# One 128x512 product per head, with its own signal, in place of four 128x256 scalings in a cross-attention stage

## The chip, the cores and the metric

The kernel runs on one core of a Trainium2 chip. The metric is the device time of one execution in microseconds (us); the median of three runs before the change is 2084.72 us (2083.55 to 2086.55).

## The reference, cut to what matters

The program is a block of four layers, each a cross attention and a feed-forward network on x of shape (8, 256, 256), with a layer norm ahead of each and a gated residual behind it. The change touches only the second layer's cross attention: 16 heads of width 64, eight batches, 256 queries and 256 keys each.

```python
def _L1_xattn_ref(x, context, mask, Wq, Wk, Wv, Wo, bo):
    q = (x @ Wq).reshape(b, n, h, d)
    k = (context @ Wk).reshape(b, m, h, d)
    v = (context @ Wv).reshape(b, m, h, d)
    sim = jnp.einsum('bihd,bjhd->bhij', q, k) * scale
    sim = jnp.where(mask[:, None, None, :], sim, neg)
    attn = jax.nn.softmax(sim, axis=-1)
    out = jnp.einsum('bhij,bjhd->bihd', attn, v)
    return out.reshape(b, n, h * d) @ Wo + bo
```

## The kernel before

The stages follow one another with a barrier of all engines between them. Inside a stage each engine has its own program, written out in full (no loop remains in this stage), and the engines meet through semaphores. An engine does its instructions in the order in which they are written, and an instruction whose semaphore isn't there yet holds up all that stand behind it.

`stage_cross_attention` works on 64 pairs of heads, 8 pairs (`PAIRS`) in each of 8 batches. For a pair g, with its two heads e_ = 0 and 1 and two tiles of 128 queries each (it = 0 and 1), the steps are:

- `scores`: TensorE forms q·k for both heads into two of the four PSUM banks `main` (line 1209). VectorE adds the mask, writes `scored` and the row maxima (line 1328, four instructions). ScalarE takes the exponential into `e` and sums each row through the accumulator into `sums` (line 1269, four instructions). `e` has the shape [128, 3, 2, 2, 256]: three slots, head, query tile, key.
- `normalise`: VectorE takes the reciprocal of the four sums (line 1336) and scales the four 128x256 blocks of `e` by them, in place (line 1341).
- `turn`: TensorE transposes the scaled weights, four 128x128 blocks a head, into the banks `turned` (line 1221); a head has a bank of its own. VectorE copies the first head's bank to `eT` (line 1350), ScalarE the second's (line 1282).
- `weigh`: TensorE multiplies by v into `av` (line 1234), VectorE copies the result to `aoT` (line 1358).

The function `walk` gives the order, the same on every engine: scores(g+1), then a slot for filler work, turn(g-1), another slot, weigh(g-2). In VectorE's program turn(g-1) ends with normalise(g), so a pair is scaled one step ahead of its transposes. The filler work of `between` belongs to neighbouring batches and is put at fixed slots: the transposes of the next batch's x in pair 0 (line 1179), its four q projections in pairs 1, 2, 4 and 5 (line 1189), the two output projections of the batch before in pairs 3 and 4 (line 1197, with the residual on VectorE at line 223), and the layer norm's last step in pair 5 (line 217). The first batch has no output projection to do, the last has no q projection.

GpSimd adds the bias to x at the start of the stage (line 1371, 16 instructions of 128x256), and then does the small steps of the layer norm (lines 182 and 185).

Of the kernel before, what the change touches and what calls it, by code (L numbers as in the profile page):

```python
# [12 lines left out]
P = 128  # L13
# [8 lines left out]
ALU = mybir.AluOpType  # L22
# [3 lines left out]
B, S, D = 8, 256, 256  # L26
# [194 lines left out]
def residual(nc, dve, core, gate, update, t, x_done):  # L221

    nc.vector.scalar_tensor_tensor(core.x[:, t, :], update, gate, core.x[:, t, :], ALU.mult, ALU.add  # L223
                                   ).then_inc(x_done, 1)
# [859 lines left out]
def stage_cross_attention(nc, core, ins):  # L1084
# [10 lines left out]
    with ExitStack() as ctx:  # L1095
# [11 lines left out]
        neg_max, sums, rsums = (st.sb(n, [P, 2, 4]) for n in ("neg_max", "sums", "rsums"))  # L1107
        e = st.sb("e", [P, 3, 2, 2, S])
# [7 lines left out]
        exp_done, recip, norm_done = st.sem("exp_done"), st.sem("recip"), st.sem("norm_done")  # L1116
# [38 lines left out]
        @block.sync  # L1155
        def _(sp):
            sp.dma_start(wo[:, :, :], ins["L1_xattn_Wo"].rearrange("(k p) n -> p k n", p=P)).then_inc(wo_in, 16)
            for b in range(1, B):
                if b >= 2:
                    sp.wait_ge(av_done, PAIRS * (b - 1))  # L1160
                sp.dma_start(kT[b % 2][:, :, :].rearrange("p k s -> p (k s)"), kv.k_list[b, :, :]
                             ).then_inc(kv_in[b % 2], 16)
                sp.dma_start(v[b % 2][:, :, :].rearrange("p h n -> p (h n)"), kv.v_list[b, :, :]
                             ).then_inc(kv_in[b % 2], 16)

        @block.tensor
        def _(pe):
# [45 lines left out]
                            last.then_inc(filled, 1)  # L1213

            def turn(g):
                pe.wait_ge(norm_done, g + 1)
                for e_ in range(2):
                    ps, filled, eT_bank[g, e_] = wt.fill()
                    for jt in range(2):
                        for it in range(2):  # L1220
                            last = nc.tensor.transpose(ps[:, jt * S + it * P:jt * S + (it + 1) * P],  # L1221
                                                       e[:, g % 3, e_, it, jt * P:(jt + 1) * P], core.ident[:, :])
                    last.then_inc(filled, 1)

            def weigh(g):
# [11 lines left out]
                last.then_inc(av_done, 1)  # L1237

            walk(scores, fill, turn, weigh)

        @block.scalar
# [55 lines left out]
        @block.vector  # L1297
        def _(dve):
            wm, wt = Walk(main, dve), Walk(turned, dve)
            dve.wait_ge(small_in, 32)  # L1300
            nc.vector.tensor_scalar(mask_add[:, :, :].rearrange("p b s -> p (b s)"), mask8[:, :], -1.0, -NEG,
                                    ALU.add, ALU.mult).then_inc(mask_ready, 1)
            dve.wait_ge(mask_ready, 1)
            nc.vector.tensor_scalar(bias[:, :], bias[:, :], tg, None, ALU.mult).then_inc(bias_ready, 1)

            def fill(b, kind, n):
                if kind == "n":
                    for h in range(2):
                        norm.vector_apply(dve, 2 * b + h, h)
                elif kind == "o":  # L1310
                    ps, empty = wm.drain()
                    if b == 0 and n == 0:
                        dve.wait_ge(bias_added, TILES)
                    residual(nc, dve, core, tg, ps[:, 0:D], 2 * b + n, x_done)
                    norm.vector_stats(dve, 2 * b + n, n, x_done)
                    core.vector_inc(empty)
                else:
                    wm.skip(1)

            def scores(g):  # L1320
                b = g // PAIRS
                if g >= 2:
                    dve.wait_ge(exp_done, 4 * (g - 1))
                for e_ in range(2):
                    ps, empty = wm.drain()
                    for it in range(2):
                        n = 2 * e_ + it
                        last = nc.vector.tensor_tensor_reduce(  # L1328
                            scored[:, g % 2, e_, it, :], ps[:, it * S:(it + 1) * S], mask_add[:, b, :], -1.0, -NEG,
                            ALU.add, ALU.min, neg_max[:, g % 2, n:n + 1])  # L1330
                    last.then_inc(empty, 1)

            def normalise(g):
                par = g % 2
                dve.wait_ge(exp_done, 4 * (g + 1))
                nc.vector.reciprocal(rsums[:, par, :], sums[:, par, :]).then_inc(recip, 1)
                dve.wait_ge(recip, g + 1)
                for e_ in range(2):
                    for it in range(2):
                        n = 2 * e_ + it  # L1340
                        last = nc.vector.tensor_scalar(e[:, g % 3, e_, it, :], e[:, g % 3, e_, it, :],  # L1341
                                                       rsums[:, par, n:n + 1], None, ALU.mult)
                last.then_inc(norm_done, 1)

            def turn(g):
                ps, empty = wt.drain()
                wt.skip(1)
                if g >= 2:
                    dve.wait_ge(av_done, g - 1)
                nc.vector.tensor_copy(eT[:, g % 2, 0, :, :].rearrange("p j s -> p (j s)"), ps[:, :]  # L1350
                                      ).then_inc(empty, 1)
                if g + 1 < ALL_PAIRS:
                    normalise(g + 1)

            def weigh(g):
                b, p = divmod(g, PAIRS)
                dve.wait_ge(av_done, g + 1)
                nc.vector.tensor_copy(aoT[:, b % 2, p, :], ps_av[g % 2][:, 0:S]).then_inc(ao_ready, 1)

            def first_scores(g):  # L1360
                scores(g)
                if g == 1:
                    normalise(0)

            walk(first_scores, fill, turn, weigh)
# [2152 lines left out]
```

## Time and profile before

| what | before |
|---|---|
| median of three runs (lowest, highest) | 2084.72 us (2083.55, 2086.55) |
| the profiled execution's own time | 2084.0 us |
| its span in the trace | 2082.3 us |
| TensorE's mean granted clock | 0.952 of full speed |
| TensorE matmul, busy | 1875.5 us, 90% |
| VectorE, busy | 1270.4 us, 61% |
| ScalarE, busy | 834.9 us, 40% |
| GpSimd, busy | 274.3 us, 13% |
| the cross-attention stage | from 317 us to 659 us of the span |

Times in the trace are counted from the start of the span. An instruction's duration runs from its start to its end, and two VectorE instructions can overlap by some hundredths of a microsecond, so the step from one start to the next is what a queue pays. In a timeline, instructions of one kind that follow each other are merged: "x4" with 1.14 us is the time from the first one's start to the last one's end. Idle time stands in brackets, with the work whose end finished it. In the names a prefix tells the stage: `ca_` is the cross attention, `f_` the feed-forward stage before it, `bt_` the last stage of the program.

### The profile page before, as it was taken

What the parts mean: (1) busy time and instruction counts of PE and PEld (TensorE: products, weight loads), DVE (VectorE), ACT (ScalarE), POOL (GpSimd) and SP (SyncE); (2) the same over time, 40 slices, a digit from 0 to 9 for tenths busy, and PEclk for the clock granted to TensorE, in tenths of its full rate; (3) what the DMA queues carried; (4) which work ended last, traced back from release to release, by engine and by line L of the source; (5) the groups of instructions that cost most, each with busy time, mean ns of one, the idle gap of its engine ahead of it and who ended that gap; (6) DMA issues with size and microseconds to landing.
All of it is one profiled execution on the core that took longest, in us unless ns stands there. A gap on an engine that the chain in (4) does not pass through costs nothing. (4 is left out here: it accounts for less than half of the span.)

```text
span 2082.3 us, 39092 instructions
## 1 busy us (share of the span) xinstructions
PE 1875.5 (90%) x13707; PEld 1518.8 (73%) x13708; DVE 1270.4 (61%) x4668; ACT 834.9 (40%) x2278; POOL 274.3 (13%) x498
## 2 busy tenths in 40 slices
PE   8899997999998989999999988997952989999978
PEld 6566665677666979999999987875531877777745
DVE  7878865877874451111111145676769529999988
ACT  3433335655552111111111101774477524444468
POOL 2001112000001070000000063331000230000022
PEclk9999999999998999999999998999975999999989
DMA  6211112111113522222222021111000031111100
GB/s 224 87 51 51 41 51 74 44 79 41 41 42 102 201 80 81 86 86 83 83 86 86 23 65 45 44 45 62 0 0 0 1 93 40 39 37 39 23 11 31
DMA packets 106722, 124.95 MB, mean 60 GB/s; under 512 B 36160, under 2 KB 85832, under 8 KB 104776
## 3 DMA queue, kind: packets, MB, share of 16 engines
q1 hardware_dynamic: 95416, 107.25, 15.6%
q0 software_dynamic: 3072, 8.39, 1.3%
q10 hardware_dynamic: 8080, 7.35, 1.1%
q8 instruction: 85, 1.39, 0.3%
q14 instruction: 69, 0.57, 0.1%
HBM read 86.39 MB, written 36.63 MB: 59 GB/s over the span
## 5 line engine op out<-in xcount | busy, mean ns | idle before, releaser
L1781 DVE TENSOR_TENSOR me_h<-me_sg,me_ps_u 128x512 f32<-128x512 f32 x106 | 72.5, 687 | 287.1 <-PE me_ps_u L1604 274.0
L1737 ACT ACTIVATE me_sg<-me_ps_g 128x512 f32<-128x512 f32 x106 | 63.3, 597 | 370.1 <-PE me_ps_g L1604 340.2
L1269 ACT ACTIVATE ca_e<-ca_scored,ca_neg_max 128x256 f32<-128x256 f32 x256 | 127.2, 499 | 108.3 <-DVE ca_neg_max L1328 108.3
L1604 PE MATMUL me_ps_g<-me_x_turned,me_w 128*128 128x128 f32 x1184 | 144.6, 275 | 1.9 <-issue 1.9
L1604 PE MATMUL me_ps_u<-me_x_turned,me_w 128*128 128x128 f32 x1184 | 144.3, 275 | 0.0
L1604 PEld LDWEIGHTS me_ps_g<-me_x_turned,me_w 128*128 128x128 f32 x1184 | 140.7, 192 | 4.5 <-issue 2.8
L1611 PE MATMUL me_ps_y<-me_w,me_h 128*128 128x256 f32 x592 | 140.0, 379 | 0.0
L1604 PEld LDWEIGHTS me_ps_u<-me_x_turned,me_w 128*128 128x128 f32 x1184 | 138.2, 192 | 0.0
L2972 ACT ACTIVATE sc_y_all<-ss_v 128x16 f32<-128x16 f32 x256 | 60.9, 238 | 156.1 <-DVE ss_v L3035 156.0
L1611 PEld LDWEIGHTS me_ps_y<-me_w,me_h 128*128 128x128 f32 x592 | 106.8, 190 | 11.4
L1328 DVE CUSTOM_DVE_ANT_0 ca_scored<-ca_main,ca_mask_add 128x256 f32<-128x256 f32 x256 | 92.8, 419 | 20.8 <-PE ca_main L1209 20.8
L3123 PE MATMUL ss_idle<-ident 128*128 128x128 f32 x648 | 90.3, 286 | 0.0
L3004 DVE SCALAR_TENSOR_TENSOR ss_left<-ss_nq,ss_v 128x16 f32<-128x16 f32 x446 | 89.8, 201 | 0.1
L1983 POOL DMA_INDIRECT me_rows<-moe_y_list,me_slot x32 | 31.2, 975 | 430.7 <-DVE carrier L81 422.5
L2392 PE MATMUL ig_ps<-nw_int_wT,ig_xT 128*128 128x384 f32 x256 | 86.7, 494 | 0.0
L3123 PEld LDWEIGHTS ss_idle<-ident 128*128 128x128 f32 x648 | 79.7, 195 | 6.5 <-issue 3.4
L2187 ACT ACTIVATE la_e<-la_scores,la_mx 128x128 f32<-128x128 f32 x256 | 70.6, 424 | 32.7 <-DVE la_mx L2229 32.7
L1805 DVE COPY me_y<-me_ps_y 128x256 f32<-128x256 f32 x37 | 15.7, 425 | 108.0 <-PE me_ps_y L1611 108.0
L1221 PE MATMUL ca_turned<-ident,ca_e 128*128 128x128 f32 x512 | 69.3, 279 | 13.3 <-DVE ca_e L1341 13.3
L1221 PEld LDWEIGHTS ca_turned<-ident,ca_e 128*128 128x128 f32 x512 | 57.1, 142 | 29.8 <-DVE ca_e L1341 22.1
L1341 DVE TENSOR_SCALAR ca_e<-ca_e,ca_rsums 128x256 f32<-128x256 f32 x256 | 74.9, 356 | 2.2
L1604 PE MATMUL me_ps_g<-me_xT,me_w13s 128*128 128x128 f32 x512 | 67.3, 284 | 5.7 <-issue 4.9
(444 smaller groups left out, 4374.4 us busy)
## 6 DMA issues: line engine op xcount, KB each, us to landing
me_w<-in_L_ffn_w_e SPq DMA_DIRECT2D x24, 1024.0 KB, 7.5
ca_k_list<-kv_out SPq DMA_DIRECT2D x28, 256.0 KB, 2.3
ca_v_list<-kv_out SPq DMA_DIRECT2D x28, 256.0 KB, 2.3
sk_gb<-scan_g_band SPq DMA_DIRECT2D x14, 512.0 KB, 3.7
moe_x_list<-me_zeros SPq DMA_DIRECT2D x1, 5248.0 KB, 21.3
me_x_tile<-moe_x_list SPq DMA_DIRECT2D x38, 128.0 KB, 2.0
moe_y_list<-me_y ACTq DMA_DIRECT2D x37, 128.0 KB, 1.7
ca_kT<-ca_k_list SPq DMA_DIRECT2D x4, 1024.0 KB, 4.9
```

Source lines behind the costliest of these rows:

```text
L1221: last = nc.tensor.transpose(ps[:, jt * S + it * P:jt * S + (it + 1) * P], e[:, g % 3, e_, it, jt * P:(jt + 1) * P], core.ident[:, :])
L1269: nc.scalar.activation(e[:, g % 3, e_, it, :], scored[:, g % 2, e_, it, :], ACT.Exp, scale=-1.0, bias=neg_max[:, g % 2, n:n + 1], accum_ou ...
L1328: last = nc.vector.tensor_tensor_reduce(scored[:, g % 2, e_, it, :], ps[:, it * S:(it + 1) * S], mask_add[:, b, :], -1.0, -NEG, ALU.add, A ...
L1341: last = nc.vector.tensor_scalar(e[:, g % 3, e_, it, :], e[:, g % 3, e_, it, :], rsums[:, par, n:n + 1], None, ALU.mult)
L1604: last = nc.tensor.matmul(ps[:, j * P:(j + 1) * P], w[:, n, kt, f:f + P], x[:, kt, :], start=(kt == 0), stop=(kt == KD - 1))
L1611: last = nc.tensor.matmul(ps_y[:, 0:D], h[:, c, j, :], w[:, f, :], start=(f == 0), stop=(f == FT - 1))
L1737: nc.scalar.activation(sg[:, c, :], ps_g[c][:, :], ACT.Silu).then_inc(done, 1)
L1781: nc.vector.tensor_tensor(h[:, c, :, :].rearrange("p j n -> p (j n)"), sg[:, c, :], ps_u[c][:, :], ALU.mult).then_inc(done[c], 1)
L2187: last = nc.scalar.activation(e[:, n % 2, r, j, :], scores.ps[r][:, j * P:(j + 1) * P], ACT.Exp, bias=mx[:, n % 2, r, j:j + 1])
L2392: last = nc.tensor.matmul(ps[2 * w + c][:, 0:HALF], xT[:, par, kt, :], wT[:, w, kt, c * HALF:(c + 1) * HALF], start=(kt == 0), stop=(kt == ...
L3004: return nc.vector.scalar_tensor_tensor(out, nq[:, t % 2, :].unsqueeze(2).broadcast_to([P, C, n]), 1.0, src, ALU.add, ALU.mult)
L3123: nc.tensor.matmul(idle[:, 0:P], core.ident[:, :], core.ident[:, :], start=True, stop=True)
```

## The change

The four scalings of a pair, each 128x256 with a scale per partition, become two products of 128x512, one for each head; the second operand is the head's two reciprocals, each read 256 times over. Each product signals `norm_done`, where before only the fourth scaling did. TensorE waits for that signal ahead of each head's transposes, where before it waited once, ahead of both.

```diff
@@ TensorE
             def turn(g):
-                pe.wait_ge(norm_done, g + 1)
                 for e_ in range(2):
+                    pe.wait_ge(norm_done, 2 * g + e_ + 1)
                     ps, filled, eT_bank[g, e_] = wt.fill()
@@ VectorE, normalise
                 for e_ in range(2):
-                    for it in range(2):
-                        n = 2 * e_ + it
-                        last = nc.vector.tensor_scalar(e[:, g % 3, e_, it, :], e[:, g % 3, e_, it, :],
-                                                       rsums[:, par, n:n + 1], None, ALU.mult)
-                last.then_inc(norm_done, 1)
+                    scale = rsums[:, par, 2 * e_:2 * e_ + 2].unsqueeze(2).broadcast_to([P, 2, S])
+                    nc.vector.tensor_tensor(e[:, g % 3, e_, :, :], e[:, g % 3, e_, :, :], scale, ALU.mult
+                                            ).then_inc(norm_done, 1)
```

VectorE's program around one `normalise`, in a pair in the middle of the stage, before. Semaphores carry the names of their first users in the program: `fa_cs_in2` is `exp_done`, `fa_cs_in3` is `recip`, `fa_cs_in5` is `av_done`.

```order
L1350 COPY ca_eT<-ca_turned 128x512 [waits fa_cs_in5,fa_ln_done]
L1336 RECIPROCAL ca_rsums<-ca_sums 128x4 [waits fa_cs_in2]
L1341 TENSOR_SCALAR ca_e<-ca_e,ca_rsums 128x256 [waits fa_cs_in3]
L1341 TENSOR_SCALAR ca_e<-ca_e,ca_rsums 128x256 x3
L1358 COPY ca_aoT<-ca_av 128x256 [waits fa_cs_in5]
```

The same place after the change.

```order
L1348 COPY ca_eT<-ca_turned 128x512 [waits fa_cs_in5,fa_ln_done]
L1336 RECIPROCAL ca_rsums<-ca_sums 128x4 [waits fa_cs_in2]
L1340 TENSOR_TENSOR ca_e<-ca_e,ca_rsums 128x512 [waits fa_cs_in3]
L1340 TENSOR_TENSOR ca_e<-ca_e,ca_rsums 128x512
L1356 COPY ca_aoT<-ca_av 128x256 [waits fa_cs_in5]
```

Two instructions stand where four stood; nothing else on VectorE is moved.

TensorE's program around one `turn`, before. Here `fa_cs_in4` is `norm_done`, and `fa_x_in1` and `fa_x_in2` tell that the banks `turned0` and `turned1` are empty.

```order
L1209 MATMUL ca_main1<-kv_kT0,ca_qT 128x256
L1221 MATMUL ca_turned0<-ident,ca_e 128x128 [waits fa_x_in1,fa_cs_in4]
L1221 MATMUL ca_turned0<-ident,ca_e 128x128 x3
L1221 MATMUL ca_turned1<-ident,ca_e 128x128 [waits fa_x_in2]
L1221 MATMUL ca_turned1<-ident,ca_e 128x128 x3
L1234 MATMUL ca_av0<-ca_eT,kv_v0 64x256 [waits fa_cs_in6,fa_x_in2,fa_x_in1]
```

And after the change.

```order
L1209 MATMUL ca_main1<-kv_kT0,ca_qT 128x256
L1221 MATMUL ca_turned0<-ident,ca_e 128x128 [waits fa_x_in1,fa_cs_in4]
L1221 MATMUL ca_turned0<-ident,ca_e 128x128 x3
L1221 MATMUL ca_turned1<-ident,ca_e 128x128 [waits fa_x_in2,fa_cs_in4]
L1221 MATMUL ca_turned1<-ident,ca_e 128x128 x3
L1234 MATMUL ca_av0<-ca_eT,kv_v0 64x256 [waits fa_cs_in6,fa_x_in2,fa_x_in1]
```

The fifth transpose, the first one of the second head, has a second semaphore to wait for; no instruction is added on TensorE.

## Rows read from the trace of the kernel before

**Rows 1.** The page: busy time of each engine over the whole span.

```profile
PE 1875.5 (90%) x13707; PEld 1518.8 (73%) x13708; DVE 1270.4 (61%) x4668; ACT 834.9 (40%) x2278; POOL 274.3 (13%) x498
```

**Rows 2.** Busy time by window, in one window of 40 us.

```profile
core 0: us, PE busy (x) PEld busy (x) DVE busy (x) ACT busy (x) POOL busy (x), PEclk, DMA share, GB/s
...
481.00:521.00 40.00, 38.96 (x259) 28.12 (x257) 31.34 (x130) 23.21 (x77) 1.49 (x4) 1.00 0.14 54
```

**Rows 3.** Waits of the stage, 317 to 660 us: total, times, longest.

```profile
DVE x_res L223 <- PE ca_main L1197: 33.0, 16, 3.8
...
DVE ca_scored L1328 <- PE ca_main L1209: 20.8, 24, 3.4
...
PE ca_turned L1221 <- DVE ca_e L1341: 13.3, 20, 2.7
```

**Rows 4.** VectorE's timeline, a middle batch: start, length, line, work.

```profile
518.65 0.69 DVE L1350 COPY ca_eT<-ca_turned 128x512 f32<-128x512 f32 x1 [0.79 <-PE ca_turned L1221]
...
519.46 1.14 DVE L1341 TENSOR_SCALAR ca_e<-ca_e,ca_rsums 128x256 f32<-128x256 f32 x4
...
527.24 1.14 DVE L1341 TENSOR_SCALAR ca_e<-ca_e,ca_rsums 128x256 f32<-128x256 f32 x4
...
530.81 1.14 DVE L1341 TENSOR_SCALAR ca_e<-ca_e,ca_rsums 128x256 f32<-128x256 f32 x4
531.87 0.42 DVE L1358 COPY ca_aoT<-ca_av 128x256 f32<-128x256 f32 x1
```

**Rows 5.** TensorE's timeline: the transposes in two successive batches.

```profile
491.59 1.09 PE L1221 MATMUL ca_turned<-ident,ca_e 128*128 128x128 f32 x8 [0.40 <-DVE ca_e L1341]
...
524.87 1.09 PE L1221 MATMUL ca_turned<-ident,ca_e 128*128 128x128 f32 x8 [0.64 <-DVE ca_e L1341]
525.89 1.08 PE L1234 MATMUL ca_av<-ca_eT,kv_v 128*64 128x256 f32 x8
...
532.01 1.09 PE L1221 MATMUL ca_turned<-ident,ca_e 128*128 128x128 f32 x8 [0.40 <-DVE ca_e L1341]
532.94 1.89 PE L1189 MATMUL ca_main<-ca_xT,kv_wq 128*128 128x256 f32 x8
```

**Rows 6.** VectorE products elsewhere in the program: two timelines.

```profile
302.65 0.89 DVE L671 TENSOR_TENSOR f_hq<-f_qh_down,f_qh_scale 128x704 f32<-128x704 f32 x1
...
2031.41 1.29 DVE L3384 TENSOR_TENSOR bt_hp<-bt_sg,bt_ps_u 128x512 f32<-128x512 f32 x2
2032.61 0.48 DVE L223 SCALAR_TENSOR_TENSOR x_res<-bt_ps_yo,bt_gate,x_res 128x256 f32<-128x256 f32 x1
```

**Rows 7.** The stage's start: timelines of four engines, and one window.

```profile
327.18 11.17 POOL L1371 TENSOR_TENSOR x_res<-x_res,ca_bias 128x256 f32 x16 [14.64 <-DVE ca_bias L1304]
...
333.44 2.96 DVE L1341 TENSOR_SCALAR ca_e<-ca_e,ca_rsums 128x256 f32<-128x256 f32 x4
...
335.06 0.57 ACT L1257 ACTIVATE ca_xT<-ca_main 128x512 f32<-128x512 f32 x1
...
336.45 1.09 PE L1221 MATMUL ca_turned<-ident,ca_e 128*128 128x128 f32 x8 [2.71 <-DVE ca_e L1341]
337.38 3.26 PE L1189 MATMUL ca_main<-ca_xT,kv_wq 128*128 128x256 f32 x8
...
338.00:339.00 1.00, 1.00 (x4) 0.81 (x3) 0.96 (x4) 1.00 (x5) 0.35 (x1) 0.50 0.00 0
```

**Rows 8.** The last batch: timelines of VectorE and TensorE.

```profile
615.22 1.14 DVE L1341 TENSOR_SCALAR ca_e<-ca_e,ca_rsums 128x256 f32<-128x256 f32 x4
...
616.42 1.09 PE L1221 MATMUL ca_turned<-ident,ca_e 128*128 128x128 f32 x8 [0.40 <-DVE ca_e L1341]
...
626.37 1.09 PE L1221 MATMUL ca_turned<-ident,ca_e 128*128 128x128 f32 x8 [0.17 <-DVE ca_e L1341]
...
636.52 1.09 PE L1221 MATMUL ca_turned<-ident,ca_e 128*128 128x128 f32 x8 [0.42 <-DVE ca_e L1341]
...
640.73 1.25 PE L1221 MATMUL ca_turned<-ident,ca_e 128*128 128x128 f32 x8 [2.11 <-DVE ca_e L1341]
```

## The prediction

> **What bounds the kernel now.** I read the page first: TensorE is busy for 90% of the span, VectorE for 61% [rows 1]. Such shares are averages over stages, so next I cut the stage that is changed into windows. In a whole window of 40 us TensorE works 38.96 us and VectorE 31.34 [rows 2]. That TensorE has about one microsecond left and VectorE almost nine says only that TensorE bounds most of a batch. The waits say where it doesn't: TensorE waits for the scaled weights 20 times, 13.3 us in all, while VectorE waits for TensorE at the residual (33.0 us) and at the scores (20.8 us) [rows 3]. So both wait, at different places, and the two timelines side by side tell which.
>
> In a middle batch VectorE waits last at 518.65. From there it runs without a gap through four groups of scalings, the first at 519.46 and the last at 530.81 [rows 4]. In that stretch TensorE is the one that waits: 0.64 us at 524.87 and 0.40 us at 532.01 [rows 5]. From 532.01 on, a q projection follows, TensorE has more to do in each pair than VectorE, and VectorE waits until the next batch's like of 518.65. The path thus lies on VectorE for about three pairs, crosses to TensorE at the transposes of 532.01, and stays there for about five. A batch takes 40.42 us (532.01 minus 491.59, the same place in two batches [rows 5]).
>
> **What the change costs on VectorE.** Four scalings take 1.14 us from first start to last end, and the next instruction starts 1.06 us after the first one (531.87 minus 530.81) [rows 4]. The trace before has no 128x512 product of two operands in SBUF. The nearest rows are the two 128x512 products with one operand in PSUM, back to back: 1.29 us from first start to last end, next instruction after 1.20 us (2032.61 minus 2031.41) [rows 6]. A product with both operands in SBUF and a repeated second one took 0.89 us for 704 columns [rows 6]; scaled down by columns with no fixed part that is 0.65 us for 512, so 0.60 to 0.70 us for one is well held. I take the two-product row: the pair costs VectorE 1.20 in place of 1.06, **+0.15 us** rounded up, the first head is ready after 0.69 us, and the second at 1.29, 0.15 us later than the signal comes now. Bounds: if the products were as fast per column as the scalings (0.26 us of step for 256 columns) nothing would be added; if they didn't overlap at all, two of 0.69 give 1.38, which adds 0.32.
>
> **What the split signal gives on TensorE.** The eight transposes take 0.93 us from the first one's start to the next work (532.94 minus 532.01) [rows 5], so 0.46 us a head. Today all 0.93 come behind the signal. After the change the first head's four go while the second product runs, and only 0.46 come behind the second signal. Where TensorE waits, it therefore ends the transposes 0.46 us sooner, less the delay of the second signal. That delay grows with the groups of scalings that VectorE has done since it last waited: with k of them, the crossing to TensorE moves by k x 0.15 - 0.46 us.
>
> The added wait itself: the fifth transpose waits for its bank already, and the eight still follow each other at an even pace, so a wait that is met costs nothing that shows. As its upper bound I take the difference between 1.02 us (525.89 minus 524.87), where a group with more waits follows, and 0.93 us [rows 5]: 0.09 us a pair.
>
> **The sum, place by place.**
> - Six middle batches, k = 4: 4 x 0.15 - 0.46 = +0.14 us each, +0.8 us.
> - The first batch's crossing has k = 3: -0.01, nothing.
> - The last batch has k = 5 at its crossing (the fifth group at 615.22, transposes at 616.42): +0.29. Then TensorE waits again for 0.17 us at 626.37, which the early first signal removes: +0.12. At 636.52 it waits 0.42; VectorE's group there is 0.12 late, so 0.12 + 0.15 - 0.46 = -0.19. One more group before 640.73 adds 0.15: -0.04 [rows 8]. About nothing.
> - The remaining groups of a batch cost VectorE 0.15 each where it waits for TensorE anyway. Their cover is the 33.0 and 20.8 us of [rows 3], nearly 7 us a batch for some 0.6 us of added work. Without that cover all 64 pairs would show: 64 x 0.15 = 9.6 us.
> - The stage's start. The first pair's four scalings take 2.96 us in place of 1.14, while GpSimd's 16 bias additions (11.17 us, 0.70 each) run beside them: 0.73 us a scaling, in step with the additions. TensorE waits 2.71 us for them and starts at 336.45 [rows 7]. Two instructions fall into that step twice, not four times. If each waits out one addition (0.70) and then takes about 0.5, the second ends 2.4 to 2.5 us after 333.44 in place of 2.96, and with 0.46 us of transposes saved behind it the q projection starts some 1.0 us sooner. Bounds: nothing, if two long products each sit through two additions; 1.7 us at most, since that projection also needs xT, which is ready at 335.63 (335.06 plus 0.57) [rows 7]. I take -1.0.
>
> The Trainium skill weighs in here: "SBUF — State Buffer", section "Who interferes with whom", says that a VectorE instruction with two SBUF inputs contends with a GpSimd instruction that reads SBUF, and that the one that comes second waits until the other is done. By it the product is held just as the scalings are, which is the step that I assume, and no gain beyond the count of instructions would come.
>
> Sum: 0.8 + 0 + 0 - 1.0 = -0.2 us. The profiled execution took 2084.0 us and would take 2083.8. The median before is 0.7 above the profiled time, so I put the forecast at 2084.72 - 0.2 = **2084.5 us**.
>
> **The rivals.**
>
> *The clock at the start stays up.* Behind the 2.71 us of idleness TensorE's granted clock fell to 0.50, that is 1.2 GHz [rows 7], and the q projection took 3.26 us where it takes 1.89 at full clock [rows 5]. With the idle time cut to about 1.0 us, then a head's transposes, then about half a microsecond, the clock may not fall: 1.4 us back there and a little behind it, -1.6 in all, 2082.9 us. For it: the waits of 0.40 to 0.64 us elsewhere leave the clock at 1.00 [rows 2]. Against: the idle time that remains is more than twice the longest of these.
>
> *Slower: the products don't overlap.* The place is VectorE's gapless stretch, the price is 0.32 us a pair. A middle batch then gets 4 x 0.32 - 0.46 = +0.82, six of them 4.9; the first crossing 0.5; the last batch about 1.1; the start gives back 1.0: +5.5, 2090.2 us. It decides from about 0.28 us a pair: with x for the price, the crossings of all eight batches make 32 x - 3.7, less 1.0 at the start, and that reaches 4.2 us there. Against: the products of [rows 6] overlap. The Trainium skill speaks for it: "VectorE: DVE Perf Modes", section "The DRAIN you can't avoid", has the next instruction wait until the pipeline is empty, and allows an earlier start only for one that isn't held. By the strict reading 2090.2 us, by the row 2084.5; the trace disagrees with the strict reading, as the second product there ends 1.29 us after the first one's start, not 1.38.
>
> *The extra wait costs on TensorE.* At the bound of 0.09 us in the five pairs of eight where TensorE sets the pace, 40 x 0.09 = 3.6: 2088.1 us. Against: the wait on the bank stands at the same instruction and shows nothing.
>
> *Faster: VectorE gets shorter.* Were the products quicker than the scalings, the gapless stretch would shrink and TensorE would never wait: at most the 13.3 us of [rows 3], less the 2 us or so that stay at the start and the end, 2074 us. No row has a float product of two tensors at that rate.
>
> *It does nothing at all*: that can't be told from the forecast, and I count it there.
>
> **How the numbers follow.** Forecast as summed 0.45; clock stays up 0.27; extra wait 0.07; no overlap or another dearer product 0.11; faster stretch 0.05; 0.05 for what I don't see. A measurement of this kernel tells about 0.2%, 4.2 us, from no change: 2080.5 to 2088.9. Within it lie the forecast, the clock and the extra wait, some 0.80 with a share of the unseen. Slower by more: 0.12. Faster: 0.08. The range leaves out the slow and the fast rival: 2081.0 to 2088.3; the forecast's own range is 2082.5 to 2087.
>
> **What would show it.** The products: 128 of them, 0.69 us each, VectorE's busy time up by some 9 us. A gapless pair: 3.57 us (from 527.24 to 530.81 [rows 4]) becomes 3.72. TensorE's wait for `ca_e`: down from 13.3 us to about half. The crossing in a middle batch: a batch of 40.42 us becomes 40.56. The start: transposes before 335.5. I would be wrong if a product lasts over 0.8 us, if GpSimd's additions hold each of them for longer than 1.5 us, or if the second head's transposes start well behind their signal.

## The result, and the profile after

| | before | change |
|---|---|---|
| median of six runs each (lowest, highest) | 2084.73 us (2083.55, 2092.56) | 2095.3 us (2092.12, 2098.64) |
| the profiled execution's own time | 2084.0 us | 2096.1 us |
| its span | 2082.3 us | 2094.0 us |

The ratio is 1.0046, interval 1.0033 to 1.0059: slower, by some 10 us, outside the forecast's range. A second session gave 1.0049 (1.0031 to 1.0066).

The page of the change answers [rows 1]: VectorE has 128 instructions fewer and 8.7 us more to do, as forecast, and TensorE is busy 10 us longer with the same number of matmuls.

```profile
PE 1885.6 (90%) x13707; PEld 1523.5 (73%) x13708; DVE 1279.1 (61%) x4540; ACT 834.3 (40%) x2278; POOL 274.6 (13%) x498
```

Now the stage that was changed. The window that answers [rows 2], the costliest group of `normalise`, and the waits that answer [rows 3]:

```profile
481.00:521.00 40.00, 39.27 (x260) 28.07 (x256) 32.29 (x111) 23.12 (x77) 1.48 (x4) 1.00 0.14 53
```

```profile
L1340 DVE TENSOR_TENSOR ca_e<-ca_e,ca_rsums 128x512 f32<-128x512 f32 x128 | 84.6, 702 | 2.2
```

```profile
DVE x_res L223 <- PE ca_main L1197: 30.9, 16, 3.8
...
DVE ca_scored L1328 <- PE ca_main L1209: 17.7, 23, 3.5
...
PE ca_turned L1221 <- DVE ca_e L1340: 9.2, 19, 2.1
```

A product takes 702 ns; TensorE's wait for `ca_e` falls from 13.3 to 9.2 us, not quite to the half that I expected. VectorE's timeline of a middle batch, which answers [rows 4]:

```profile
526.66 1.29 DVE L1340 TENSOR_TENSOR ca_e<-ca_e,ca_rsums 128x512 f32<-128x512 f32 x2
...
530.39 1.29 DVE L1340 TENSOR_TENSOR ca_e<-ca_e,ca_rsums 128x512 f32<-128x512 f32 x2
531.60 0.42 DVE L1356 COPY ca_aoT<-ca_av 128x256 f32<-128x256 f32 x1
```

Two products last 1.29 us, the next instruction starts after 1.21 (531.60 minus 530.39), and a gapless pair lasts 3.73 us (530.39 minus 526.66): forecast 1.29, 1.20 and 3.72. TensorE's timeline, which answers [rows 5] and [rows 8]:

```profile
490.54 1.26 PE L1221 MATMUL ca_turned<-ident,ca_e 128*128 128x128 f32 x8 [0.39 <-DVE ca_e L1340]
...
531.13 1.26 PE L1221 MATMUL ca_turned<-ident,ca_e 128*128 128x128 f32 x8 [0.39 <-DVE ca_e L1340]
532.23 1.89 PE L1189 MATMUL ca_main<-ca_xT,kv_wq 128*128 128x256 f32 x8
...
625.92 1.09 PE L1221 MATMUL ca_turned<-ident,ca_e 128*128 128x128 f32 x8
...
635.62 1.25 PE L1221 MATMUL ca_turned<-ident,ca_e 128*128 128x128 f32 x8
```

A batch takes 40.59 us (531.13 minus 490.54) where it took 40.42: forecast 40.56. In the last batch two of the three small waits are gone. At the stage's start (timelines of VectorE and TensorE and one window, against [rows 7]):

```profile
334.33 2.21 DVE L1340 TENSOR_TENSOR ca_e<-ca_e,ca_rsums 128x512 f32<-128x512 f32 x2
```

```profile
335.47 0.66 PE L1221 MATMUL ca_turned<-ident,ca_e 128*128 128x128 f32 x4 [0.83 <-DVE ca_e L1340]
336.60 0.66 PE L1221 MATMUL ca_turned<-ident,ca_e 128*128 128x128 f32 x4 [0.48 <-DVE ca_e L1340]
337.10 1.89 PE L1189 MATMUL ca_main<-ca_xT,kv_wq 128*128 128x256 f32 x8
```

```profile
338.00:339.00 1.00, 1.00 (x7) 0.62 (x5) 0.97 (x3) 1.00 (x4) 1.00 (x2) 1.00 0.00 0
```

The granted clock stays at 1.00, 2.4 GHz, where it was 0.50: the q projection takes 1.89 us, not 3.26. The changed stage as a whole is 2.5 us *shorter*. So the time is lost elsewhere. I cut both traces at the stages' borders. The cross attention is counted from the last work of the stage ahead of it, each later part from its own first work, and the rest ends with TensorE's last matmul (us):

```
                      ahead   cross att.  mixture of e.  local att.  rest
before                312.5   346.47      629.30         154.20      636.09
change                313.2   343.97      635.12         161.55      636.52
difference             +0.7    -2.50       +5.82          +7.35       +0.43
```

All of the loss lies in stages that the diff doesn't touch. What differs there? The records of TensorE's sequencer hold 852 semaphore instructions before and 915 after: 63 more. The fifth transpose of each pair but the first waits for two semaphores, and for the second one a separate instruction is put ahead of it. TensorE's program is 63 instructions longer, and all that follows lies that much further on.

In local attention, the waits that end with "issue", that is with nothing that the profile shows, before and then after the change; a larger one that is the same in both (`la_scores`, 15.2 us) is left out:

```profile
PEld la_turned L2131 <- issue: 5.3, 6, 1.6
...
PEld la_av L2148 <- issue: 1.5, 8, 0.3
```

```profile
PEld la_turned L2129 <- issue: 9.4, 10, 1.8
...
PE la_turned L2129 <- issue: 3.6, 4, 1.7
PEld la_av L2146 <- issue: 2.9, 9, 1.4
...
PE la_av L2146 <- issue: 1.2, 1, 1.2
```

TensorE's matmuls never wait in this way before, and 4.8 us after the change (3.6 and 1.2), out of the 7.35 us by which the stage is longer. Another 2.6 us are matmul time: 142.89 us busy after, 140.28 before.

TensorE's timeline at one such place, before and then after the change. In each case the rows close a burst of 128 short matmuls that began 2.0 us earlier.

```profile
1326.61 0.41 PE L2148 MATMUL la_av<-la_eT,la_vz 128*32 128x64 f32 x16
1326.83 0.41 PE L2148 MATMUL la_av<-la_eT,lp_ones 128*32 128x64 f32 x16
1327.17 1.09 PE L2131 MATMUL la_turned<-ident,la_e 128*128 128x128 f32 x8
```

```profile
1332.37 0.41 PE L2146 MATMUL la_av<-la_eT,la_vz 128*32 128x64 f32 x16
1332.59 0.41 PE L2146 MATMUL la_av<-la_eT,lp_ones 128*32 128x64 f32 x16
1334.66 1.09 PE L2129 MATMUL la_turned<-ident,la_e 128*128 128x128 f32 x8 [1.66 <-issue]
```

The same instruction starts without a gap before, and 1.66 us late after. TensorE's own code comes through a DMA queue. Queue and window of that stage before:

```profile
q8 instruction: 24, 0.39, 1.2%
```

```profile
1288.00:1441.00 153.00, 140.28 (x2980) 113.15 (x2980) 106.16 (x186) 105.24 (x330) 52.47 (x90) 0.94 0.15 41
```

24 transfers bring 0.39 MB, 16 KB each, for 5960 weight loads and matmuls, 248 to a transfer besides semaphores and the like: some 64 bytes for each instruction. A burst of 128 matmuls with their weight loads eats one transfer's worth in 2.0 us, while the stage's mean is one per 6.4 us. The Trainium skill, "Runtime: NRT & Kernel Launch", section "Instruction fetch mechanics", says that code comes in blocks of 16 KiB, 256 instructions, and that crossing a border is mostly hidden. The trace agrees on the size. If the stalls above are such crossings, it disagrees with the second part behind dense bursts.

**The theory** then: 63 added instructions (4032 bytes, about a quarter of a block) move the borders through the later stages, and the loss is the place of the code, not the work of the change. **The rivals:** the second wait costs by itself; the products do; or the later stages' lengths are scatter.

### The profile page after: what moved, and what is told of

Same layout as the page of the kernel before. It is cut to its first block and busy times, and to the rows that moved or that the text cites. A ratio compares the mean times of both kernels' runs of the same rounds, so it can differ in the third digit from the quotient of the medians.

```text
span 2094.0 us, 39027 instructions
## 1 busy us (share of the span) xinstructions
PE 1885.6 (90%) x13707; PEld 1523.5 (73%) x13708; DVE 1279.1 (61%) x4540; ACT 834.3 (40%) x2278; POOL 274.6 (13%) x498
## 3 DMA queue, kind: packets, MB, share of 16 engines
q10 hardware_dynamic: 8080, 7.35, 1.1%
## 5 line engine op out<-in xcount | busy, mean ns | idle before, releaser
L1340 DVE TENSOR_TENSOR ca_e<-ca_e,ca_rsums 128x512 f32<-128x512 f32 x128 | 84.6, 702 | 2.2
```

Of the source, the lines that this page charges most:

```text
L1340: nc.vector.tensor_tensor(e[:, g % 3, e_, :, :], e[:, g % 3, e_, :, :], scale, ALU.mult).then_inc(norm_done, 1)
```

## The experiments

Diffs are against before unless it is said otherwise, and each group of kernels is compared with runs of before taken beside it.

**Undoing one part at a time.** Only the wait is doubled, on the same value, the scalings stay:

```diff
             def turn(g):
-                pe.wait_ge(norm_done, g + 1)
                 for e_ in range(2):
+                    pe.wait_ge(norm_done, g + 1)
```

> The kernel before, with one thing added: TensorE waits for norm_done a second time, ahead of the second head's transposes, for the value that it has already seen. VectorE is as before. It adds 63 semaphore instructions to TensorE's program (852 to 915, as the change did) and nothing else. Theory A, the loss of the change comes from TensorE's program being 63 instructions longer, so that the later stages' instruction fetches fall elsewhere: cross attention unchanged (317 to 657.2 us), the mixture-of-experts and local-attention stages together some 10 us longer, about 2095. Theory B, it comes from what VectorE does or from VectorE's program being 128 instructions shorter: 2084.7, no change.

Measured: 1.0031 (1.0018 to 1.0043), 2093.86 us. Cross attention takes 346.33 us, as before, so the wait is free where it stands; TensorE waits 13.2 us for `ca_e`, as before; the later stages are 13.3 us longer. The profiled execution (2099.46 us) is the longest of the twelve, so these 13.3 us overstate the loss: by the medians it is 6.5 to 7.4 us. The added instructions alone bring most of the loss, or all of it: the change's interval, 1.0033 to 1.0059, overlaps this one.

The change, but without an added instruction: TensorE asks for the second bank at the second transpose, which waits for nothing else, so that each waits for one semaphore (against the change):

```diff
             def turn(g):
+                pe.wait_ge(norm_done, 2 * g + 1)
+                (ps0, filled0, eT_bank[g, 0]) = wt.fill()
                 for e_ in range(2):
-                    pe.wait_ge(norm_done, 2 * g + e_ + 1)
-                    ps, filled, eT_bank[g, e_] = wt.fill()
+                    if e_ == 1:
+                        pe.wait_ge(norm_done, 2 * g + 2)
                     for jt in range(2):
                         for it in range(2):
+                            if e_ == 0 and (jt, it) == (0, 1):
+                                (ps1, filled1, eT_bank[g, 1]) = wt.fill()
+                            ps, filled = (ps0, filled0) if e_ == 0 else (ps1, filled1)
```

> The changed kernel, but TensorE waits for the second head's bank to be empty at its second transpose of the first head, so that the second head's norm_done wait is the only one at the fifth: the 63 extra semaphore instructions are gone, TensorE's program has the length of before. The products and their two signals stay. Theory A (the length of TensorE's program): cross attention ends near 655.4 us as in the changed kernel, the later stages take what they took before, about 2082.5. Theory B (VectorE's program or its products): about 2095, as the changed kernel.

Measured: 0.9993 (0.9978 to 1.0007), 2085.94 us; 852 semaphore instructions, local attention 154.82 us, cross attention 343.71. Everything that the change does to VectorE is in it, and the loss is gone.

The products with one signal behind the second, and one wait:

```diff
-                    for it in range(2):
-                        n = 2 * e_ + it
-                        last = nc.vector.tensor_scalar(...)
+                    scale = rsums[:, par, 2 * e_:2 * e_ + 2].unsqueeze(2).broadcast_to([P, 2, S])
+                    last = nc.vector.tensor_tensor(e[:, g % 3, e_, :, :], e[:, g % 3, e_, :, :], scale, ALU.mult)
                 last.then_inc(norm_done, 1)
```

> The products of the change with the signal of before: only the second product signals, TensorE waits once ahead of both heads. TensorE's program is that of before. Theory A: later stages as before; the crossing of a middle batch moves by 4 x 0.15 = +0.6 us in place of +0.14, seven or eight of them +4.5 us, less some 0.5 to 2 at the start, so 2087 to 2089. Theory B: the same and another 10 us, about 2098.

Measured: 1.0018 (1.0003 to 1.0033). Cross attention takes 348.39 us, and TensorE waits for `ca_e` longer than before:

```profile
PE ca_turned L1221 <- DVE ca_e L1340: 17.2, 22, 2.3
```

Four scalings, a signal behind the second and the fourth, and TensorE's part as in the folded kernel:

```diff
                     for it in range(2):
                         n = 2 * e_ + it
                         last = nc.vector.tensor_scalar(...)
-                last.then_inc(norm_done, 1)
+                    last.then_inc(norm_done, 1)
```

> The four scalings of before, with a signal behind the second and one behind the fourth, and TensorE's waits placed as in the folded kernel, so that its program keeps its length. The first head is ready 0.61 us after the first scaling's start, the second at 1.14. Theory A: each crossing to TensorE comes up to 0.46 us sooner, eight of them some 3.5 us, with 1 us or less at the start: about 2081, and later stages as before. Theory B says nothing else here; if the early signal were worth nothing it would be 2084.7.

Measured: 0.9982 (0.9968 to 0.9996), 2083.3 us: this one beats both kernels. TensorE's wait for `ca_e`, half of that before:

```profile
PE ca_turned L1226 <- DVE ca_e L1346: 6.4, 12, 2.0
```

**Moving the code alone.** At the end of TensorE's part of the stage come 16, 32 or 64 short products that nobody reads; each stands as two weight loads and two matmuls, so they fill 4, 8 and 16 KB by the 64 bytes worked out above; one semaphore instruction comes with them. The last shifts everything by a whole block, which should undo itself.

```diff
             walk(scores, fill, turn, weigh)
+            wt.when_all_read()
+            for _ in range(16):
+                nc.tensor.matmul(turned.ps[0][:, 0:64], core.ident[:, :], core.ident[:, 0:64], start=True, stop=True)
```

> The kernel before, with 16 small float products (128x64, of the identity matrix, into a PSUM bank that is no longer used, read by nobody) at the end of TensorE's program of the cross-attention stage, where TensorE waits for the barrier. Each is two weight loads and two matmuls in the program, so 32 pairs of instructions are added, about as many bytes as the 63 semaphore instructions of the change. Theory A (where the blocks of TensorE's program fall in the later stages): local attention longer than its 154.2 us, by 4 to 8 us, as with the extra waits. Theory C (the extra waits themselves cost, in place): local attention stays at 154 us, the whole at the time of before.

> As the kernel with 32 added pairs of TensorE instructions, but 64 pairs. Theory A: local attention has some other length, between 152 and 163 us; no value is foretold. Theory C: 154 us.

> As before, but 128 added pairs of TensorE instructions: in long even stretches of the trace one fetch of 16384 bytes comes for each 128 to 129 pairs, so this moves all later code by one whole block. Theory A in the form that blocks lie on a fixed grid: local attention is back at 154.2 us, within 1 us. If it is longer by 4 us or more, the place within a block isn't what decides. Up to 1 us more in cross attention, for the added work.

Then the change with 48 such products, 12 KB, which with its own 4 KB make one block (the same lines, against the change):

> The changed kernel with 96 added pairs of TensorE instructions at the end of cross attention: with its 63 semaphore instructions this makes one whole block. Theory A with a fixed grid: local attention falls from 161.6 us back to about 154.5 and the whole to about 2087 to 2089. Theory C or any theory by which the products or the waits slow what follows: 161 us stays, 2095.

Measured, with the padding itself counted in the cross-attention stage (us):

```
                     ratio (95%)               cross att.  mixture of e.  local att.  rest
4 KB                 1.0048 (1.0030, 1.0067)   347.34      630.71         158.16      640.15
8 KB                 1.0078 (1.0061, 1.0095)   348.12      631.57         168.48      636.89
16 KB                1.0058 (1.0039, 1.0077)   359.00      630.92         154.16      637.07
change and 12 KB     1.0041 (1.0026, 1.0055)   351.61      629.13         154.86      635.91
```

Local attention goes from 154.2 us to 158.2, to 168.5, and back to 154.2 when the shift is a whole block, though no instruction of that stage is touched. With 8 KB TensorE stalls inside a burst, ahead of its 96th matmul of 128; the timeline and the waits show it:

```profile
1333.25 0.22 PE L2151 MATMUL la_av<-la_eT,lp_ones 128*32 128x64 f32 x1 [2.06 <-issue]
```

```profile
PEld la_av L2151 <- issue: 14.4, 15, 2.2
PE la_av L2151 <- issue: 11.8, 7, 2.1
```

The trace ties these stalls to the code transfers. Here TensorE goes on at 1333.25, and the last 16 KB transfer of q8 had landed at 1331.77, 1.48 us earlier. TensorE's matmuls stall for over 1 us with "issue" 23 times in local attention, counted past its first 5 us and over all twenty profiles. All 23 lie in the nine profiles with a shift of 4 or 8 KB, and each ends 1.2 to 1.6 us behind the landing of a 16 KB transfer. The eleven others have none.

And the change with 12 KB has all three parts behind the cross attention back at their lengths of before: 1419.9 us together, before 1419.6, the change 1433.2. Its added waits are still there, so it isn't they that cost.

The expectations were wrong on the price of the padding, and the whole time can't carry this reading. The 128 added matmuls take 14.40 us and the 96 take 10.83, of which the wait for the barrier hides only 2 to 3, so the padding costs 12.5 us in its own stage with 16 KB, where 1 us more was expected, and 7.6 us in the change with 12 KB. That kernel was expected at 2087 to 2089 us and took 2094.0, and its ratio of 1.0041 can't be told from the change's 1.0046. Its profiled execution, 2090.22 us, was the second shortest of nine. What shows the return is the stages' lengths.

**Again, for the scatter.** Before and the change, two more profiles of each:

> The kernel before once more, for a second profile. In the profiles so far the mixture-of-experts stage took 629.3 us before and from 629.1 to 637.6 in nine others, without a rule in the length of either program. If that is a scatter from one execution to the next, a second profile of the same kernel may land anywhere in that range; local attention, if it is set by the place of the program's blocks alone, stays at 154.2.

> The changed kernel once more. Local attention stays near 161.6 us if the place of the blocks alone sets it; if it comes out near 158.7, as in the kernel with the waits alone, the 2.9 us between them are scatter. The mixture-of-experts stage: 635.1 us again if the change is the cause, anywhere from 629 to 638 if it is scatter.

> A third profile of the kernel before, as e9: local attention 154.2 us, mixture of experts 629 if it is steady, else anywhere up to 638.

> A third profile of the changed kernel, as e10: cross attention 344.0 us, local attention between 158.5 and 161.6, mixture of experts 635 if the change is the cause.

Measured: before 2083.93 and 2083.76 us, and 2091.51 in one more execution that has no profile; the change 2102.19 and 2096.88. So before alone varies by 7.8 us from one execution to the next. Mixture of experts 630.19 and 632.62 against 640.44 and 633.47; local attention 154.65 and 154.62 against 158.62 and 158.91; the rest 635.30 and 635.47 against 640.45 and 640.17. Two things came out. In the third profile of before the clock did not fall at the stage's start, after nearly as long a wait as in [rows 7]:

```profile
335.67 1.09 PE L1221 MATMUL ca_turned<-ident,ca_e 128*128 128x128 f32 x8 [2.46 <-DVE ca_e L1341]
336.60 1.89 PE L1189 MATMUL ca_main<-ca_xT,kv_wq 128*128 128x256 f32 x8
```

That profile's cross attention takes 343.59 us, as short as the change's. The whole execution is no shorter for it: its mixture of experts takes 632.62 us, where the second profile of before has 346.23 and 630.19, and the sums are 976.2 and 976.4. The clock shows where these 2.4 us go. The mean granted clock over the first 24 us of that stage (third number from the end) is 0.72 in the first and second profiles of before, and 0.60 in its third. It is 0.59 in the change, and 0.60 in the folded kernel. Before, before's third profile, and the change:

```profile
659.00:683.00 24.00, 23.19 (x150) 22.96 (x151) 1.88 (x6) 8.04 (x14) 6.26 (x22) 0.72 1.02 320
```

```profile
656.00:680.00 24.00, 23.40 (x128) 23.14 (x127) 1.20 (x5) 7.88 (x13) 5.91 (x21) 0.60 1.04 328
```

```profile
657.00:681.00 24.00, 23.20 (x122) 22.97 (x123) 1.19 (x5) 8.22 (x13) 6.24 (x22) 0.59 1.02 319
```

And the 4 us of the rest lie at the start of the state-space stage, where the clock rises later. Windows of TensorE's first 40 us there, before and in the change's third profile (the granted clock is the third number from the end):

```profile
1712.00:1732.00 20.00, 14.62 (x77) 12.08 (x78) 15.29 (x114) 7.78 (x34) 0.00 (x0) 0.74 0.12 31
1732.00:1752.00 20.00, 18.69 (x136) 15.51 (x135) 19.66 (x147) 8.46 (x43) 0.00 (x0) 1.00 0.13 35
```

```profile
1720.00:1740.00 20.00, 14.55 (x62) 12.36 (x63) 14.57 (x109) 7.03 (x31) 0.00 (x0) 0.57 0.11 30
1740.00:1760.00 20.00, 19.44 (x120) 16.08 (x118) 16.03 (x119) 6.89 (x35) 0.00 (x0) 0.83 0.09 30
```

Six repeats in a later session, in which before itself took 2069.82 and 2070.17 us. It has no profile there, and the mixture of experts is some 13 to 17 us shorter in every kernel than in the first session, so the stage times that the expectations name for it can't be held against these; kernels are compared within the session:

> The kernel before with the doubled wait on TensorE, a second time, to see whether its mixture-of-experts stage is again long. If that stage follows the place of TensorE's program or the doubled wait, its profile shows 635 to 640 us there, as in the first profile (637.58); if that first profile was scatter of the stage, 629 to 633. The local-attention stage is expected at 158 to 162 us by the theory of the place in either case, and the ratio at 1.002 to 1.005.

> The kernel before with 32 pairs of padding, a second time. By the theory of the place the local-attention stage is again 158 to 162 us. If the mixture-of-experts stage follows the place of TensorE's program, it should be 635 or more at least in this profile; if it follows the doubled wait alone, again 630 to 632.

> The change without an added TensorE instruction, a second time. Local attention 154 to 155 us. The mixture-of-experts stage 629 to 633 us if what lengthens it is the added waits or the place of the program; 635 or more would put the blame on the changed work of VectorE itself. Ratio 0.998 to 1.001.

> Four scalings with two signals and the bank's wait moved to the second transpose, timed again with more rounds, since it was the fastest. If the earlier ratio of 0.9982 is real, the same again, 0.997 to 0.9995; if it was scatter, 0.9990 to 1.0005. Stages: cross attention 343.5 us, mixture of experts 629 to 633, local attention 154 to 155.

> The change with 12 KB of padding, which puts the later stages' TensorE code back on the grid of before, a second time. If all of the late loss follows the place of the program, mixture of experts, local attention and the rest together take within 2 us of what they take in before on the same chip (1419.6 us on the first chip, about 1407 on the second), and the ratio is that of the cross-attention stage alone, about 1.003 to 1.004. If the added waits or the shorter VectorE program lengthen the mixture-of-experts stage by themselves, it is 3 to 8 us longer than that again.

> The change itself beside it on the same chip. The theory of the place expects the three parts behind the cross attention to be 9 to 16 us longer than in the padded kernel: 4 to 7 us in local attention, 0 or 4.5 us at the start of the state-space stage, where the clock rises later, and 2 to 8 us in the mixture of experts. The rival, in which the padding changes nothing behind local attention, expects 4 to 7 us in all. Ratio to before 1.003 to 1.006.

```
                     ratio (95%)               cross att.  mixture of e.  local att.  rest
waits only           1.0045 (1.0029, 1.0060)   348.12      620.24         159.30      637.43
4 KB                 1.0057 (1.0041, 1.0072)   347.47      616.83         157.98      636.96
folded wait          0.9994 (0.9983, 1.0006)   343.87      618.09         154.23      636.66
scalings, split      0.9984 (0.9975, 0.9993)   339.21      615.58         154.23      636.60
change and 12 KB     1.0033 (1.0022, 1.0044)   351.55      616.55         154.53      636.93
change               1.0049 (1.0031, 1.0066)   344.87      619.79         159.08      637.69
```

Every verdict repeats, though the intervals of the change and of its padded form overlap (1.0031 to 1.0066, and 1.0022 to 1.0044). The change with 12 KB is 8.6 us shorter behind the cross attention than the change beside it (1408.0 against 1416.6), 4.6 of it in local attention, 3.2 in the mixture of experts and 0.8 in the rest. The scalings with a split signal are again the fastest, 0.16% below before. Local attention behaved as the theory of the place expected in all repeats. With scalings and a split signal cross attention took 339.21 us, not 343.5, with the clock up at its start this time.

The mixture of experts as a whole did not answer cleanly: in the first padded 4 KB kernel and in its repeat it is as short as elsewhere. One stretch of it does, where the shared expert ends and the loop over the routed ones begins. TensorE's timeline there, before and then after the change:

```profile
791.30 0.41 PE L1617 MATMUL me_ps_x<-ident,me_x_tile 128*128 128x128 f32 x2
793.60 2.05 PE L1604 MATMUL me_ps_g<-me_x_turned,me_w 128*128 128x128 f32 x16 [1.89 <-issue]
```

```profile
793.49 0.41 PE L1615 MATMUL me_ps_x<-ident,me_x_tile 128*128 128x128 f32 x2 [0.91 <-DMA me_x_tile<-moe_x_list]
795.85 3.40 PE L1602 MATMUL me_ps_g<-me_x_turned,me_w 128*128 128x128 f32 x16 [1.94 <-issue]
```

The stretch from the start of the shared expert's last 16 matmuls (line 1611 before) to the routed experts' first matmul of the same line takes 13.00 us before, 15.76 after the change and 15.89 with 4 KB of padding alone. In the later session it takes 19.17 to 19.31 us in the three kernels with a 4 KB shift and 16.98 to 17.27 in the three others. In the first session the two groups overlap (13.0 to 17.4 us in five profiles, 11.6 to 15.1 in eight).

## Why the prediction was wrong

The step that failed is the one on the added wait: "a wait that is met costs nothing that shows", with its bound of 0.09 us a pair, and the words ahead of it that no instruction is added on TensorE. The bound was sought only at the instruction itself, and there it holds: with the waits alone cross attention took 346.33 us in the first profile, before 346.47, and TensorE waited for `ca_e` as long as before in both (13.2 and 13.3 us). The repeat took 348.12 us; there the granted clock was 0.50 for 6.8 us at the start, where before had 3.4. What I left out is that a second semaphore on one instruction is an instruction of its own in TensorE's program, 63 of them, and that the code behind them moves against the borders of its 16 KB blocks. With the waits alone that was worth 6.5 and 9.3 us (1.0031 and 1.0045), none of it in the stage in the first session; in the second up to 1.7 us may lie there. My slower rivals looked for a price per pair in the stage, and "what I don't see" got 0.05.

Where the loss lies:
- Local attention: 158.0 to 161.6 us in all eight profiles with a 4 KB shift, 153.5 to 154.9 in all eleven without a shift or with a whole block. Shown: it follows the place. The change itself had 161.55 us and then 158.62 and 158.91, so some 3 us within the shifted ones are scatter.
- The start of the state-space stage, 0 or some +4.5 us. It came in three of those eight profiles (two of the change, one of padding alone) and in none of the other twelve. That it comes with the place is indicated; why only in some executions stays open.
- The mixture of experts: 633.5 to 640.4 us in four profiles with the added waits against 629.3 to 632.6 in three of before. It has three parts.
  - Its start, 2.9 us in the change's first profile, is the clock and not the place: the third profile of before and the folded kernel have 2.8 us of it. In before's third profile it takes back most of what the clock gained in the cross attention.
  - The entry to the routed experts, 2.8 us in that profile (15.76 against 13.00), follows the place by about 2 us in the later session, with padding alone too; the first session only points that way. These two parts make the 5.8 us of the change's first profile.
  - Another 5 us or more came in two of the eight shifted profiles (the waits alone, and the change's second), 100 to 118 us into the stage. TensorE starves there with nothing shown that it waits for, while GpSimd's indirect transfers run:

```profile
768.42 0.59 PE L1602 MATMUL me_ps_u<-me_xT,me_w13s 128*128 128x128 f32 x3 [0.70 <-issue]
769.86 0.50 PE L1602 MATMUL me_ps_u<-me_xT,me_w13s 128*128 128x128 f32 x3 [0.84 <-issue]
...
772.00 0.46 PE L1609 MATMUL me_ps_y<-me_w2s,me_h 128*128 128x256 f32 x1 [1.05 <-issue]
```

  That is the change's second profile. The four other profiles of kernels with the waits and both with 4 KB of padding have at most 1.1 us there, as kernels without a shift do; the kernel with one signal and the 8 KB one have 2.5 to 2.7. Whether it is late code stays open.

What held, term by term:
- **The products.** 702 ns for 0.69 us, 1.21 for 1.20 to the next instruction, 8.7 us more on VectorE for some 9. The overlap forecast from [rows 6] is there, and the rival without it fell.
- **The crossings.** k x 0.15 - 0.46 gave +0.14 for a middle batch; measured +0.17 (40.59 against 40.42). It also gives the other two kernels. With one signal nothing is taken off: 32 x 0.15 = 4.8 us, measured 348.39 against 343.59, 4.8, both with the clock up at the start. That the two agree to a tenth is in part luck, since the stage's start, 0.6 us shorter with the products, isn't in the 4.8. With scalings and a split signal k x 0.15 is absent: 8 x 0.46 = 3.7 us less; measured 343.48 against 346.47, 3.0, both with the clock down there; with it up in both, 339.21 in the later session against 343.59 in the first, 4.4. So the split signal gains, the products lose, and together they cancel.
- **The start.** The two products took 2.21 us, for 2.4 to 2.5 forecast, and the first half of the transposes began at 335.47. Counted from the stage's first work, the q projection began 0.94 us sooner (1.0 forecast). The rival of the clock came true, nearly always: the first q projection took 1.89 us in seven of eight profiles with products and a split signal, but in only two of nine with scalings and one signal (before's third, and the 8 KB one), else 3.1 to 3.6. So these 2.5 to 2.9 us are a likelier outcome, not a sure gain, and 2.8 us or more went again at the start of the mixture of experts in seven of the eleven profiles that had kept the clock. Idle time alone doesn't decide it: scalings with a split signal had 1.23 and then 0.35 us of it and lost the clock in one profile (q projection 3.62 us), and had 1.27 and 0.81 us and kept it in the other (1.89).
- **The sum in the stage.** With the clock up, the change and its folded form took 343.6 to 344.0 us in five profiles, against 343.59. The forecast of about nothing for the edit's own work was right: the folded kernel, which is the change without its accident of place, measured 0.9993 and 0.9994 where the forecast of 2084.5 means 0.9999. For the whole program that is in part luck: in the folded kernel's first profile the cross attention is 2.8 us shorter than before, with the clock up, which the forecast didn't count, and the mixture of experts is 3.9 us longer.

## What to carry to other kernels

- Count the instructions of each engine's program, semaphore ones included, before and after an edit; a second wait on an instruction adds one. Let a neighbour that waits for nothing take it: here that was worth about 0.5% (1.0046 against 0.9993), more than the edit's own effect.
- If a stage that you didn't touch changes its length, look there for idle time that ends with "issue" behind dense bursts of short instructions, and pad the program to see whether the loss comes and goes with a whole block.
- Price a signal's place and an instruction's length apart. The better half alone (four scalings, signal after two) gives 0.9982 and 0.9984.

## What was not expected of the hardware

- The place of TensorE's code within 16 KB blocks is worth up to 14 us in a stage of 154 (154.2, 158.2, 168.5 and 154.2 us at shifts of 0, 4, 8 and 16 KB). A burst of 128 short matmuls with their weight loads uses up a block in 2.0 us, and all 23 stalls of over 1 us end 1.2 to 1.6 us behind the landing of a block.
- Two 128x512 products of SBUF operands beside GpSimd's additions take 2.21 us, 1.29 without them.
- After 2.71 and 2.55 us of idleness the clock fell to 0.50 in the q projection behind the stage's first transposes in two profiles of before (3.26 and 3.15 us), and after 2.46 us it stayed up in the third (1.89 us). The same kernel then began the next stage 2.8 us slower, so a clock that stays up in one stage needn't shorten the whole.
